# Attention over 64 graphs on one core: a second PSUM bank for weighing the last group's values, outputs written over the residual, and a new order behind the loop

## The reference, cut to what matters

```python
h = jnp.maximum(_layernorm(x, axis=-1), 0.0)        # x: 64 graphs x 128 nodes x 384
q = _heads(h @ Wq + bq)                              # 6 heads of 64
k = _heads(h @ Wk + bk)
v = _heads(h @ Wv + bv)
scores = jnp.einsum('bhqd,bhkd->bhqk', q, k) / np.sqrt(64)
bias = jnp.where(adj, 0.0, NEG)[:, None]
probs = jax.nn.softmax(scores + bias, axis=-1)
ctx = jnp.einsum('bhqk,bhkd->bhqd', probs, v)        # heads joined again to 384
x = x + (ctx @ Wf + bf)
```

## Time and profile before

| What | Before |
| --- | --- |
| median of 3 runs (lowest to highest) | 472.5 us (472.2 to 472.67) |
| the profiled execution's own time | 471.44 us |
| its span, first to last instruction | 469.7 us |
| TensorE's granted clock, mean | 0.996 |
| PE, DVE, ACT, POOL busy | 459.9, 367.2, 363.7, 303.5 us |

### The profile page before, as it was taken

The page is one execution under the profiler, slowest core; times in us unless marked ns, Lnnn a source line. Parts: engine busy times, 40 slices in busy tenths (PEclk is TensorE's granted clock), DMA queues, the critical chain, the costliest instruction groups (busy, mean ns, idle before and its releaser), DMA issues.

```text
span 469.7 us, 12877 instructions
## 1 busy us (share of the span) xinstructions
PE 459.9 (98%) x4457; PEld 273.7 (58%) x4457; DVE 367.2 (78%) x742; ACT 363.7 (77%) x816; POOL 303.5 (65%) x308
## 2 busy tenths in 40 slices
PE   6999999999999999999999999999999999999986
PEld 2755656566575655646556574655647566565653
DVE  6989889859988685967869687686977788687963
ACT  3889999865987778868778887778878877867940
POOL 3378578683876765666766576775667476634861
PEclk8999999999999999999999999999999999999999
DMA  8256789989899696977969599694969979776994
GB/s 295 70 122 138 145 126 192 207 137 210 190 168 214 109 219 133 209 178 146 211 120 224 115 195 204 122 222 77 210 153 177 223 111 182 167 109 151 161 189 158
DMA packets 219615, 78.56 MB, mean 167 GB/s; under 512 B 199472, under 2 KB 219568, under 8 KB 219568
## 3 DMA queue, kind: packets, MB, share of 16 engines
q1 hardware_dynamic: 209200, 65.63, 72.2%
q10 hardware_dynamic: 10368, 12.33, 9.2%
HBM read 16.19 MB, written 12.58 MB: 61 GB/s over the span
## 4 chain that ended last, share of the span: by engine, by line
PE 90%; SPq 5%; DVE 2%; DMA 1%; issue 1%; POOL 0%; ACT 0%; DVEq 0%; ACTq 0%
PE ps_proj L999 25%; PE ps_proj L1001 25%; PE ps_proj L1000 25%; PE ps_scores L1064 7%; PE ps_ctx L999 2%; PE ps_ctx L1000 2%; PE ps_ctx L1001 2%; SPq L571 2%; SPq L563 2%; DMA y<-y_sb 1%; DMA x_sb<-in_x 1%; PE ps_proj L1130 1%; SPq L553 0%; DVE stats L808 0%; PE ps_scores L999 0%
## 5 line engine op out<-in xcount | busy, mean ns | idle before, releaser
L643 POOL TENSOR_TENSOR probs_parts<-probs,probs_parts 128x768 f16<-128x768 f32 x64 | 105.3, 1648 | 31.2 <-ACT probs_parts L758 31.0
L743 ACT ACTIVATE probs<-masked,neg_max 128x128 f32<-128x128 f32 x384 | 118.3, 389 | 5.8 <-POOL x_bf L638 4.1
L999 PE MATMUL ps_proj<-ht_parts,w_hi 128*128 128x512 f16 (+1 forms) x309 | 109.6, 360 | 0.4 <-DVE qkt_lo L843 0.4
L1001 PE MATMUL ps_proj<-ht_parts,w_lo 128*128 128x512 f16 (+1 forms) x309 | 109.6, 360 | 0.0
L1000 PE MATMUL ps_proj<-ht_parts,w_hi 128*128 128x512 f16 (+1 forms) x309 | 109.6, 360 | 0.0
L727 ACT ACTIVATE qkt_hi<-ps_proj,bias_qk 128x512 f16<-128x512 f32 x94 | 63.2, 681 | 39.1 <-PE ps_proj L1001 38.6
L649 POOL TENSOR_TENSOR ctx_parts<-ctx_sb,ctx_parts 128x384 f16<-128x384 f32 x62 | 56.8, 918 | 52.6 <-ACT ctx_parts L764 52.6
L843 DVE SCALAR_TENSOR_TENSOR qkt_lo<-ps_proj,bias_qk,qkt_hi 128x512 f16<-128x512 f32 x94 | 68.6, 741 | 26.7 <-ACT qkt_hi L727 26.7
L628 POOL TENSOR_TENSOR h_pairs<-h_sb,h_pairs 128x384 f16<-128x384 f32 x60 | 54.5, 916 | 40.3 <-ACT h_sb L718 40.1
L862 DVE SCALAR_TENSOR_TENSOR masked<-ps_scores,score_unscale,mask 128x384 f32<-128x384 f32 x128 | 72.4, 609 | 8.5 <-PE ps_scores L1064 8.3
L638 POOL TENSOR_TENSOR x_bf<-x_sb,b_out 128x384 f32<-128x384 f32 x64 | 63.0, 1000 | 5.9 <-DVE y_sb L894 4.2
(11 more groups left out here) (104 smaller groups left out, 911.6 us busy)
## 6 DMA issues: line engine op xcount, KB each, us to landing
y<-y_sb SPq DMA_DIRECT2D x64, 192.0 KB, 2.5
x_sb<-in_x ACTq DMA_DIRECT2D x56, 192.0 KB, 3.2
x_sb<-in_x SPq DMA_DIRECT2D x8, 192.0 KB, 5.6
pt_parts<-probs_parts SPq DMA_TRANSPOSE x64, 4.0
ct_parts<-ctx_parts SPq DMA_TRANSPOSE x62, 2.8
adj_sb<-in_adj ACTq DMA_DIRECT2D x14, 64.0 KB, 3.7
w_raw<-in_Wk SPq DMA_DIRECT2D x1, 576.0 KB, 6.3
w_raw<-in_Wv SPq DMA_DIRECT2D x1, 576.0 KB, 7.4
```

Of the source, the lines that this page charges most:

```text
L643: nc.gpsimd.tensor_tensor(probs_parts[b][:, 1, :], probs[b % 2][:], probs_parts[b][:, 0, :], ALU.subtract).then_inc(probs_split, 1)
L743: last = nc.scalar.activation(probs[b % 2][:, u * N:(u + 1) * N], masked[b % 2][:, u, :], ACT.Exp, bias=neg_max[b % 2][:, u:u + 1])
L999: nc.tensor.matmul(to, a_hi, b_hi, start=first, stop=False)
L1001: return nc.tensor.matmul(to, a_lo, b_hi, start=False, stop=last)
```

## The change

Three edits in code and a new table of turns for groups 7 to 15:

- Graphs 15.1 and 15.3 are weighed into bank 2 of the scores instead of `ps_ctx`. PE's wait before weighing 15.1 becomes the masking of the last scores, before 15.2 and 15.3 the `normalize_ctx` two graphs back.
- `finish` of groups 14 and 15 writes its output over the residual in `x_bf`, from where it is stored; it no longer waits for a store.
- The turns of groups 7 to 15 behind the loop are replaced. On every engine the same items run as before, up to the loop's end in the same order.

```diff
+def output_in_place(group):
+    return group >= GROUPS - 2
+
+def second_ctx(group, b):
+    return group == GROUPS - 1 and b % 2 == 1
...
-        def weighted(b):
-            return ps_ctx[0][:, 0:HEADS * E].rearrange("p (h e) -> p h e", h=HEADS)
+        def weighted(g, b):
+            ps = ps_scores[:, 1024:1536] if second_ctx(g, b) else ps_ctx[0]
+            return ps[:, 0:HEADS * E].rearrange("p (h e) -> p h e", h=HEADS)
...
+        def output(g, b):
+            return x_bf[g % 2][:, b, :] if output_in_place(g) else y_sb[b][:]
...
-                sp.dma_start(out_v[g + 2 * i, :, b, :], y_sb[b][:]).then_inc(y_stored[b], 16)
+                sp.dma_start(out_v[g + 2 * i, :, b, :], output(g, b)).then_inc(y_stored[b], 16)
...
-                if g >= 1:
+                if g >= 1 and not output_in_place(g):
                     dve.wait_ge(y_stored[b], by_group(g - 1, i))
-                nc.vector.scalar_tensor_tensor(out=y_sb[b][:], in0=proj("project_out", g, b)[:, 0:H],
+                nc.vector.scalar_tensor_tensor(out=output(g, b), in0=proj("project_out", g, b)[:, 0:H],
...
-                if g >= 1 or b >= 1:
+                if g == GROUPS - 1 and b == 1:
+                    pe.wait_ge(scores_masked, B * GROUPS)
+                elif g == GROUPS - 1 and b >= 2:
+                    pe.wait_ge(ctx_normalized, nth(B, g, b - 2, i))
+                elif g >= 1 or b >= 1:
                     pe.wait_ge(ctx_normalized, nth(B, g, b - 1, i))
```

`weighted(b)` becomes `weighted(g, b)` in `normalize_ctx` and `weigh_values`. Of the table, the entries for groups 13 and 15 that the text below speaks of:

```diff
     13: {
-        "finish": (-28430, -28300, -28210, -28140), "store": (-29290, -29260, -29200, -29150),
+        "finish": (-28300, -28290, -28220, -28170), "store": (-29240, -29140, -29130, -29120),
...
     15: {
-        "load": (-49010, -48940, -48840, -48800), "load_mask": (-48580,),
+        "load": (-48840, -48810, -48800, -48770), "load_mask": (-48980,),
...
-        "weigh_values": (-48820, -48800, -48770, -48740), "normalize_ctx": (-48130, -48100, -48080, -48030),
+        "weigh_values": (-48810, -48790, -48760, -48750), "normalize_ctx": (-48110, -48090, -48060, -48050),
...
```

More of the change, by code:

```diff
@@ L149 @@
     7: {
-        "store": (20194, 28042, 29836, 30000),
+        "store": (20194, 28042, 29836, 30030),
     },
     8: {
-        "transpose_ctx": (14976, 17114, 18843, 20020), "project_out": (18234, 19476, 20070, 20110),
-        "finish": (19635, 20030, 20160, 20200), "store": (20010, 20100, 20130, 20140),
-    },
-    9: {
[L157 to L163, removed]
+        "transpose_ctx": (14976, 17114, 18843, 20020), "project_out": (18234, 19476, 20020, 20160),
@@ L164 @@
     },
     10: {
[L166 to L174, removed]
+        "project_qk": (0, 10, 40, 50, 60, 70), "qk_hi": (0, 30, 60, 100, 110, 120),
+        "qk_lo": (70, 90, 110, 120, 140, 150), "project_v": (80, 110, 120, 130), "values_hi": (160, 180, 200, 210),
@@ new lines @@
+        "values_lo": (220, 240, 250, 260), "residual": (0, 10, 40, 130), "scores": (100, 150),
+        "mask_scores": (160, 170, 270, 360), "largest_score": (180, 290, 300, 380),
+        "exponentials": (220, 240, 270, 350), "probs_hi": (230, 280, 340, 380), "probs_lo": (140, 160, 190, 200),
+        "transpose_probs": (90, 140, 150, 230), "weigh_values": (240, 290, 370, 410),
+        "normalize_ctx": (430, 520, 650, 690), "ctx_hi": (400, 560, 610, 660), "ctx_lo": (220, 320, 340, 370),
+        "transpose_ctx": (180, 250, 290, 310), "project_out": (360, 460, 470, 510), "finish": (600, 810, 830, 860),
@@ L175 @@
+        "store": (370, 380, 390, 440),
     },
     11: {
[L177 to L190, removed]
+        "statistics": (-16803, -14830, -9990, -9980), "aggregate": (-9960,), "inverse_deviation": (-9970,),
+        "shift": (-9920,), "normalize": (-9950, -9930, -9860, -9850), "normed_lo": (-9940, -9930, -9910, -9900),
@@ new lines @@
+        "exponentials": (-9530, -9470, -9460, -9350), "probs_hi": (-9490, -9450, -9360, -9310),
+        "probs_lo": (-9710, -9670, -9650, -9620), "transpose_probs": (-9760, -9720, -9700, -9640),
+        "weigh_values": (-9560, -9520, -9480, -9390), "normalize_ctx": (-9200, -9180, -9050, -8950),
+        "ctx_hi": (-9250, -9190, -9090, -9050), "ctx_lo": (-9550, -9530, -9490, -9480),
+        "transpose_ctx": (-9660, -9650, -9590, -9540), "project_out": (-9400, -9360, -9330, -9280),
+        "finish": (-8970, -8910, -8860, -8780), "store": (-9550, -9460, -9440, -9430),
@@ L191 @@
     },
     12: {
[L193 to L207, removed]
+        "load": (-19960, -19910, -19810, -19740), "statistics": (-19800, -19790, -19680, -19660),
@@ L208 @@
+        "ctx_hi": (-19020, -18930, -18890, -18700), "ctx_lo": (-19460, -19370, -19350, -19290),
+        "transpose_ctx": (-19530, -19470, -19410, -19400), "project_out": (-19270, -19130, -19090, -19060),
+        "finish": (-18770, -18550, -18480, -18420), "store": (-19420, -19330, -19310, -19260),
     },
     13: {
-        "load": (-29540, -29510, -29460, -29430), "load_mask": (-29190,),
-        "statistics": (-29400, -29370, -29330, -29290), "aggregate": (-29270,), "inverse_deviation": (-29630,),
@@ L212 @@
[L212 to L222, removed]
@@ L223 @@
[L223 to L225 removed]
+        "load": (-29640, -29480, -29430, -29420), "load_mask": (-29710,),
+        "statistics": (-29370, -29360, -29300, -29290), "aggregate": (-29280,), "inverse_deviation": (-29640,),
+        "shift": (-29240,), "normalize": (-29290, -29280, -29270, -29260),
@@ L226 @@
+        "transpose_ctx": (-29370, -29360, -29290, -29280), "project_out": (-28960, -28950, -28910, -28890),
+        "finish": (-28300, -28290, -28220, -28170), "store": (-29240, -29140, -29130, -29120),
     },
     14: {
[L228 to L235, removed]
-        "additive_mask": (-38520,), "residual": (-39330, -39190, -39180, -39120), "scores": (-39090, -39040),
-        "mask_scores": (-38510, -38480, -38440, -38420), "largest_score": (-38490, -38460, -38410, -38390),
@@ L243 @@
-        "finish": (-38110, -38060, -38050, -38040), "store": (-39110, -39100, -39090, -39080),
+        "load": (-39370, -39240, -39200, -39160), "load_mask": (-39230,),
+        "statistics": (-39230, -39100, -39030, -39020), "aggregate": (-39010,), "inverse_deviation": (-39510,),
+        "shift": (-38960,), "normalize": (-39030, -38970, -38950, -38920),
+        "normed_lo": (-39450, -39440, -39420, -39410), "transpose_normed": (-39520, -39510),
+        "project_qk": (-39220, -39210, -39190, -39180, -39160, -39150),
@@ L261 @@
-        "finish": (-48020, -48000, -47980, -47970), "store": (-49070, -49060, -49050, -49040),
-        "turn_ctx": (-48750, -48720), "turned_ctx_hi": (-48240, -48230), "turned_ctx_lo": (-48010, -47990),
+        "load": (-48840, -48810, -48800, -48770), "load_mask": (-48980,),
+        "statistics": (-48700, -48670, -48660, -48650), "aggregate": (-48630,), "inverse_deviation": (-49300,),
+        "shift": (-48610,), "normalize": (-48720, -48710, -48670, -48660),
+        "normed_lo": (-49280, -49270, -49260, -49250), "transpose_normed": (-49390, -49380),
```

83 lines of the change are left out of this document (62 added, 21 removed).

## The result

| What | Before | After |
| --- | --- | --- |
| median of 5 runs (lowest to highest) | 472.5 us (472.02 to 472.67) | 469.83 us (469.57 to 470.04) |
| the profiled execution's own time | 471.44 us | 469.91 us |
| its span | 469.7 us | 468.2 us |

The ratio of the times is 0.9947, with an interval of 0.9927 to 0.9967: the change makes the kernel faster, by 2.7 us between the medians.

The account below looks back on a forecast made before the run. PE bounds the kernel, busy 459.9 of 469.7 us; of 4.2 us idle, 0.3 + 0.4 + 0.1 + 0.5 + 0.7 = 2.0 stays, gaining 2.2: 471.44 becomes 469.2, plus 1.1 to the median, 470.3. Range 469.0 to 472.4.

Parts of the forecast that it names:

- the likeliest case: Whole kernel: the forecast itself, a median of 470.3 us, given a chance of 0.60.
- four signs of being right: Finish 15.0 without store wait; shift 0.15 us; weighing 15.3 21.5 to 22.8 us after group 15's first scores; idle near 0.8.
- Idle that can be won: PE behind the loop: 3.8 us idle from group 15's first scores on, with 0.37 earlier 4.2 us.
- Behind T: From the start of group 15's first scores (T): PE waits 0.3 at weighing 15.3, 0.4 at turn 15.2, 0.1 at out 14.2.
- the last transpose: Transposed probabilities of 15.3 land at T + 21.5 to 22.5, PE comes at T + 21.8: wait 0 to 0.7, taken 0.3.
- Ahead of T: Loop's end to group 15's first scores: 0.5 us for group 14's first scores, 0.7 for the rest of the new order.
- The shift: DVE's shift of group 15: 0.15 us with POOL idle; beside a probs_lo the sum would be up to 1.5 us worse.
- The outputs in place: Finishes of groups 14 and 15 lose their wait for a store; only one was late, by 2.45 us.
- The second bank: Weighing 15.3 waits only for normalize_ctx 15.1; the new wait ahead of weighing 15.1 costs nothing.
- the load was not late (first): Rival: late load of 15.3 makes group 14's first scores wait 1.3 instead of 0.5 us; 471.1 us, chance 0.17.
- the slower one: Rival: eleven stores pile up behind the last transpose, the last landing 3.9 us late; 474.2 us, chance 0.09.
- The second: Rival: SP's transposes stay as late, probabilities 15.3 landing at T + 24.5, PE waiting 2.7 us; 472.5 us, chance 0.12.

Follow-up runs that it names:

- e0: The kernel before, unchanged, run and profiled once more: 472.47 us, ratio 1.0009 to before.
- e5: The changed kernel with ctx_hi 14.1 moved on ACT behind values_hi 14.3 and the exponentials of 15.0: 468.54 us, ratio 0.9939 to before.
- e7: The changed kernel, nothing altered, run and profiled once more: 469.86 us, ratio 0.9968 to before.
- e1: The kernel before with only the outputs of groups 14 and 15 in place, old order, no second bank: 470.71 us, ratio 0.998 to before.

## Why the prediction was right, point by point

The time, 470.3 forecast and 469.83 measured, was right within half a microsecond, and the likeliest case was the one that came. Its terms fell less well, and that the number came so close is in part luck: idle behind T was 1.9 us more than forecast, idle ahead of T 1.2 less, and the 1.1 added at the end is no constant. Of its four signs of being right two came (finish 15.0 without a wait, the shift) and two did not: weighing 15.3 started at T + 24.45, not by T + 22.8, and PE's idle time behind T was 2.7, not near 0.8.

- **Idle that can be won** (4.2 us): right for the execution it was read from; e0 has 5.1 by the same account. e5, with nearly all of it taken out, shows 29.76 from T to the last product's result by the same account; less the 28.8 of work that leaves 1.0 idle, where the prediction had 0.8 for after.
- **Behind T**, predicted idle 0.3 + 0.4 + 0.1 = 0.8; measured 31.54 - 28.8 = 2.7 in after, 2.2 in e7. The step that failed is in the working of the last transpose: "DVE: mask 15.2 1.1 ... ACT: exponentials 1.85". It followed ACT only from the exponentials of 15.2 on, as though ACT came there on time. The queue ahead of them, with a ctx_hi in it that waits for a transpose, was left out. That put probs_hi 15.3 at T + 17.9 instead of T + 16.3, the landing at T + 24.4 instead of T + 21.5 to 22.5, and weighing 15.3 at T + 24.45. With that wait moved (e5) the predicted times hold: exponentials of 15.3 follow, probs_hi ends at T + 16.3, weighing 15.3 starts at T + 22.7, inside the window that the prediction gave.
- **The bank of v 15.3** has no term in the working behind T (that all other products find their data early is said of the stretch ahead of T). PE waited 1.31 there for the values_lo of 15.1: the same delay on ACT; in e5 the wait is gone.
- **Turn 15.2** was to wait 0.4 for normalize_ctx 15.2: it did not in after, because weighing 15.3, ahead of it, came later. Out 14.2 was to wait 0.1 for its bank: 0.23.
- **Ahead of T**, predicted 0.5 for a late load of 15.3 and 0.7 for the rest of the order, after 0.37 won: measured no wait at all and T half a microsecond earlier. The load was issued at 396.48 rather than 397.8 and the loads there landed in 2.9 us rather than 4.0 (a transfer row below); the last qk_lo ended at 408.50 and PE came to the scores at 408.96, as predicted within 0.2. The 0.7 was a bound without a row, and too careful.
- **The shift**, 0.15 with POOL idle: measured 0.16, and POOL had nothing between rstd and a ctx_lo at 407.22. The Trainium skill, SBUF — State Buffer, section Who interferes with whom, says that a DVE instruction with two SBUF inputs contends with a GpSimd instruction that reads SBUF; by that the row agrees (0.16 with POOL idle).

DVE's timeline of after, shift, last qk_lo and finish:

```profile
403.67 0.16 DVE L838 SCALAR_TENSOR_TENSOR shift_by<-moments,rstd 128x4 f32<-128x4 f32 x1 [1.19 <-POOL rstd L628]
...
407.75 0.75 DVE L857 SCALAR_TENSOR_TENSOR qkt_lo<-ps_proj,bias_qk,qkt_hi 128x512 f16<-128x512 f32 x1 [1.90 <-ACT qkt_hi L741]
...
459.38 1.74 DVE L908 SCALAR_TENSOR_TENSOR x_bf<-ps_proj,y_unscale,x_bf 128x384 f32<-128x384 f32 x3
```

POOL's, and the loads of x_sb from 385 to 420:

```profile
407.22 0.91 POOL L663 TENSOR_TENSOR ctx_parts<-ctx_sb,ctx_parts 128x384 f16<-128x384 f32 x1 [3.58 <-ACT ctx_parts L778]
...
455.80 5.78 POOL L652 TENSOR_TENSOR x_bf<-x_sb,b_out 128x384 f32<-128x384 f32 x6
```

```profile
DMA to landing us min/median/max: 2.5/2.9/3.5
```

- **The outputs in place**: right that the finish of 15.0 follows without a wait for a store (the x3 above are 14.2, 14.3 and 15.0 back to back), and e1 prices that in the old order at 1.5 us by the medians and 0.9 by the ratio (with an interval that just reaches no change). Six residuals on POOL were hidden, as said.
- **The second bank**: its new wait costs nothing, as predicted; its gain, which the prediction did not price apart, is none that shows in the old order and about 0.7 in the new one.
- **The base.** The sum went against the profiled execution of before, and 1.1 us was added to reach the median. After's profiled execution lies on its median (469.91 and 469.83). The 1.1 was thus no constant around the span. By e0, most of it is waits for late transposes that the first execution of before happened not to have; the one for the context of 14.1 is in none of the five profiles of the new order, while what e0 lost ahead of the loop's end can befall both kernels. Two executions do not show how often. Read against the profile, the sum was 0.7 too hopeful (469.2 against 469.91); read against the median, 0.5 too careful.

The rivals: the load was not late (first), and the slower one did not come: eleven stores left from 458.31 to 466.2, and the end followed the last product at the same distance as before. The second, transposes as late as before, came nearest: probabilities of 15.3 did land at T + 24.4, as before at T + 24.5. It did not cost its full price because PE had spent 1.31 of that time already in waiting for v 15.3, and because the gains ahead of T and in finish 15.0 do not hang on that transpose. Its reason was not in the main the one given, SP's places, but ACT: the low half was ready only at 453.08, and SP sent it 0.27 later, where in e5 and e7 it took 0.1.

## What to carry to other kernels

When an order is moved, follow each queue from its last known wait, not from the item that matters: a wait that is harmless on its own engine (here ctx_hi behind a buffer's last reader) holds up all that stands behind it, and moving that one entry brought 1.3 us more, at least half of what the whole change had. An edit may be worth something only with another: a second bank paid nothing that shows in the old order and about 0.7 in the new. And profile the kernel before twice before a median is set against one execution: what differed between the two here was mostly waits for transfers.
